# A graph-convolution kernel on one core: a 23rd tile slot, one buffer of x instead of two, and the kept tiles stated per column band

## What is computed

```python
A = adj + eye(8192)
deg = sum(A, axis=1)
d = rsqrt(deg)
h = (A * d[:, None] * d[None, :]) @ x
out = layernorm(x + elu(h @ w))
```

## Time and profile before

| | |
|---|---|
| median of three runs | 1066.4 us |
| the profiled execution's own time | 1068.32 us |
| its span on the core | 1066.5 us |
| TensorE (PE) busy | 926.0 us, 87% |
| VectorE (DVE) busy | 765.1 us, 72% |
| ScalarE (ACT) busy | 711.9 us, 67% |
| read from HBM | 364.2 MB, 345 GB/s over the span |
| loads of adj | 338, of 1 MB each, all by SyncE's queue (SP) |
| loads of x into the scaling buffer | 21 |

### The profile page before, as it was taken

How to read it: one execution, slowest core, us unless ns; L and a number is a source line. 1 busy time by engine, 2 the same in 40 slices (tenths; PEclk the granted TensorE clock), 3 DMA queues, 4 the chain that set the end, 5 groups by cost and what they waited for, 6 DMA issues and landing times.

```text
span 1066.5 us, 35050 instructions
## 1 busy us (share of the span) xinstructions
PE 926.0 (87%) x15744; PEld 846.4 (79%) x15744; DVE 765.1 (72%) x633; ACT 711.9 (67%) x1693; POOL 196.2 (18%) x268
## 2 busy tenths in 40 slices
PE   0089399499597998998989899999999999999995
PEld 0086189399596997798889888979989999999994
DVE  0587587566766767787777677989998785866933
ACT  6898898888988889898988979850226828100201
POOL 0210120300402103041230444474001100000000
PEclk9999799699898999999899999999999999999998
DMA  9999999999999999999999999979997998999930
GB/s 378 397 387 412 395 397 403 394 398 401 397 397 400 393 377 400 379 395 389 389 391 374 394 394 345 337 257 372 302 301 268 287 304 278 291 328 311 357 111 21
DMA packets 170903, 370.66 MB, mean 348 GB/s; under 512 B 6272, under 2 KB 33536, under 8 KB 161536
## 3 DMA queue, kind: packets, MB, share of 16 engines
q1 hardware_dynamic: 153856, 360.01, 91.7%
q10 hardware_dynamic: 16896, 8.39, 2.7%
HBM read 364.18 MB, written 4.19 MB: 345 GB/s over the span
## 4 chain that ended last, share of the span: by engine, by line
PE 45%; issue 40%; DMA 6%; POOL 5%; ACT 2%; DVE 1%; SPq 1%; POOLq 0%; DVEq 0%; ACTq 0%
PE p_set L883 44%; DMA space<-in_adj 6%; POOL space L769 3%; ACT space L786 1%; PE p_set L861 1%; DMA xn<-in_x 1%; POOL xn L762 1%; POOL rstd L776 1%; POOL space L750 0%; SPq L731 0%; POOL d L756 0%; DVE space L914 0%; ACT space L794 0%; DVE hT L925 0%; ACT L786 0%
## 5 line engine op out<-in xcount | busy, mean ns | idle before, releaser
L883 PE MATMUL p_set<-space 32*128 32x256 f32 (+2 forms) x15616 | 909.6, 391 | 127.3 <-ACT space L794 61.0
L883 PEld LDWEIGHTS p_set<-space 32*128 32x128 f32 x15616 | 831.0, 188 | 201.6 <-issue 144.9
L901 DVE STREAM_TRANSPOSE space<-space 128x2048 f32<-128x2048 f32 x256 | 582.2, 2296 | 119.4 <-ACT space L786 75.1
L786 ACT ACTIVATE space<-space 128x512 f32<-128x512 f32 (+2 forms) x744 | 578.7, 779 | 82.8 <-DMA space<-in_adj 78.8
L925 DVE TENSOR_TENSOR hT<-p_set,hT 128x1024 f32<-128x1024 f32 (+1 forms) x108 | 104.2, 986 | 136.0 <-PE p_set L883 135.9
L809 ACT ACTIVATE space<-space 128x512 f32<-128x512 f32 x16 | 10.1, 629 | 199.9 <-DVE space L936 199.8
L786 ACT ACTIVATION_READ_ACCUMULATOR space<-space 128x1 f32 x744 | 138.9, 187 | 0.0
L769 POOL COPY space<-xn 32x512 f32<-32x512 f32 x192 | 120.5, 628 | 11.9
L756 POOL TENSOR_TENSOR d<-deg,half 128x4 f32<-128x4 f32 x16 | 16.3, 1018 | 542.6 <-DVE deg L907 542.6
L794 ACT ACTIVATE space<-xn 32x512 f32<-32x512 f32 x112 | 70.3, 627 | 43.9 <-POOL xn L762 35.3
L776 POOL TENSOR_TENSOR rstd<-var_eps,half 128x4 f32<-128x4 f32 x16 | 16.5, 1031 | 279.8 <-DVE var_eps L970 279.7
(11 more groups left out here) (16 smaller groups left out, 29.8 us busy)
## 6 DMA issues: line engine op xcount, KB each, us to landing
space<-in_adj SPq DMA_DIRECT2D x338, 1024.0 KB, 13.0
xn<-in_x SPq DMA_DIRECT2D x21, 256.0 KB, 12.7
space<-in_x ACTq DMA_DIRECT2D x16, 256.0 KB, 5.8
out_rows<-space ACTq DMA_DIRECT2D x16, 256.0 KB, 7.3
w_sb<-in_w SPq DMA_DIRECT2D x1, 64.0 KB, 1.8
```

The lines of the kernel that those rows point to most:

```text
L786: ins = nc.scalar.activation(view[:, g], view[:, g], ACT.Copy, accum_out=to[:, g:g + 1])
L883: ins = nc.tensor.matmul(to, xs_chunk(h, j)[quadrant(q)], moving, start=first and s == b == 0, stop=last and s == b == 3)
L901: nc.vector.transpose(slots[slot], slots[slot]).then_inc(tile_turned, 1)
```

## The change

The planner's constants and two places of the program change:

- SLOTS 22 to 23, and XN 2 to 1: one more slot of 8 KB per partition, one buffer of x (2 KB per partition) less.
- The kept tiles are stated per column band, always the ones nearest the diagonal. It adds tiles (6,2), (6,3) and (8,5): 57 kept instead of 54, so 79 tiles are loaded again instead of 82.
- WIDTHS (2,) to (4, 2): a group of four kept tiles side by side, loaded in four pieces of 128 rows x 2048 columns, where five slots are free and four of them adjacent.
- STAY 11 to 10 (band 10 keeps its home; homes are loaded 20 times, not 21), FEED 12 to 14, FLIGHT 5 to 4, and the costs that the planner counts with.
- w is loaded over the identity matrix, before the ninth "again" tile, when all 16 diagonals are done (`sp.wait_ge(diagonal_added, BANDS)`), no longer first of all; TensorE waits for it before the first product with w.

```diff
-SLOTS = 22
+SLOTS = 23
-KEEP = (12, 10, 8)
+KEPT = (1, 2, 3, 4, 5, 6, 5, 4, 4, 4, 5, 4, 1, 2, 3, 4)
-STAY = 11
-WIDTHS = (2,)
-XN = 2
+STAY = 10
+WIDTHS = (4, 2)
+XN = 1
-FEED = 12
-FLIGHT = 5
+FEED = 14
+W_AFTER = 8
+FLIGHT = 4
...
 def kept_units():
+    return {(t, u) for t in range(BANDS) for u in range(t + 1 - KEPT[t], t + 1)}
...
-    FAR, NEAR, XLOAD, LAND = 2.5, 2.68, 0.9, 2.0
+    FAR, MID, NEAR, XLOAD, LAND = 2.57, 2.65, 2.73, 1.0, 2.0
...
-            offer("pool", 3, "scale", home_of[t], 1.35)
+            offer("pool", 3, "scale", home_of[t], 1.15)
...
-                offer(e, 0 if some is FIRST_COPIES else 4, "copies", (arg, i), {"dve": 0.43, "act": 0.64, "pool": 0.8}[e] * len(pairs))
+                offer(e, 0 if some is FIRST_COPIES else 4, "copies", (arg, i), {"dve": 0.65, "act": 0.64, "pool": 0.72}[e] * len(pairs))
...
-                    kind, long = "part", took(len(parts[arg][2]))
+                    kind, long = "part", took(len(parts[arg][2])) + (1.75 if now - until["pe"] > 2.5 else 0.0)
...
-        w_sb = sb("w_sb", [F, F])
+        w_sb = ident
...
-            sp.dma_start(w_sb[:, :], w).then_inc(w_loaded, 16)
+            agains = [arg for what, arg in order["sp"] if what == "load" and loads[arg][:2] == ("tile", "again")]
             for what, arg in order["sp"]:
+                if what == "load" and arg == agains[W_AFTER]:
+                    sp.wait_ge(diagonal_added, BANDS)
+                    sp.dma_start(w_sb[:, :], w).then_inc(w_loaded, 16)
...
                 elif kind == "copies":
                     h, some = arg
                     pool.wait_ge(x_scaled, scale_nth[h])
+                    diagonals_before = sum(k == "diagonal" for k, _ in order["pool"][:order["pool"].index((kind, arg))])
+                    if diagonals_before:
+                        pool.wait_ge(diagonal_added, diagonals_before)
...
-            pe.wait_ge(w_loaded, 16)
             for kind, arg in order["pe"]:
                 if kind == "out":
+                    if not arg:
+                        pe.wait_ge(w_loaded, 16)
```

More of the change, by code:

```diff
@@ L261, in issue @@
             wide = load[5] * (BAND if load[0] == "near" else 1) if load[0] != "tile" else BAND
-            dma = max(dma, now + 1.0) + (FAR if wide == 2048 else NEAR - 0.1 if wide >= 1024 else NEAR)
+            dma = max(dma, now + 1.0) + (FAR if wide == 2048 else MID if wide >= 1024 else NEAR)
             events.append((dma + LAND, k, "landed", k))
@@ L321, in finished @@
             known.add(arg)
-            offer("pool", 0, "scale", home_of[arg], 1.35)
+            offer("pool", 0, "scale", home_of[arg], 1.15)
             if arg in held_diagonals:
```

## The result

The changed kernel takes 1060.79 us (median of seven runs, 1058.63 to 1063.25) against 1066.40 us: ratio 0.996, interval 0.9947 to 0.9972. It is faster by 4.3 us by the ratio and by 5.6 us by the medians, where 11.9 were forecast. The profiled execution took 1063.25 us, the slowest of the seven, with a span of 1061.5.

The account below looks back on a forecast made before the run. Loads were taken to bound the kernel until 596 us, TensorE afterwards. 1068.3 - 10.4 (kept tiles) - 1.5 (wide pieces) = 1056.4 us for the profiled execution, 1.9 us over the median, so 1054.5 us was forecast, range 1042 to 1071.

Parts of the forecast that it names:

- The reading of the bound: Whole kernel: loads set the pace until 596 us, then TensorE alone; its work left at the last wait sets the end.
- the walked start of band 9: TensorE, band 9: starts at 596.6 us, without a wait and without the slow clock.
- the walk: TensorE's timeline, bands 6 to 9, with three more kept tiles: followed band by band, 10.4 us saved.
- The buffer of x: Loads of x, end of pass one: at most 25 us late, hidden by TensorE's backlog, cost 0.
- the 10.4 counted for them: Bands 6 and 8: three more kept tiles, multiplied before band 9, save 10.4 us.
- First product with w after 749: nothing.: Pass two: w's later load, behind an "again" load issued at about 734.5 us, costs nothing.
- the loads unmoved: Before band 8: d at 549.32 us and home 8 not ready before 555.29, loads taken as unmoved.
- Cost **0: Slots while strips 2 to 7 pass: one slot less shortens the load queue from five to four, cost 0.
- the wait that was forecast before band 8: TensorE before band 8: wait grows from 2.76 to 4.2 us and the slow clock stays, 3.1 us.
- The wide pieces: Near loads before band 9: up to 32 wide pieces, 0.09 us each, at most 2.9 us; 1.5 us taken.
- I take 0, between +5 and the gain of the first rival: Load order: FEED, FLIGHT, STAY and the planner's costs only reorder loads; effect taken as 0.
- the first rival: Waits after band 4: all five go with their slow clock, 24.2 us gained, 1042 us; chance 0.13.

Follow-up runs that it names:

- w_front: The changed kernel with w in a place of its own, loaded first of all, queue orders unchanged: 1057.67 us, ratio 0.9914 to the kernel before.
- before_x1: The kernel before with one buffer of x in the program alone, order still planned for two: 1084.14 us, ratio 1.0159.
- w_front_kept54: w_front with the 54 kept tiles of the kernel before, order planned anew: 1067.55 us, ratio 1.0039 to the kernel before.
- narrow_held: w_front with each group of four wide pieces loaded as four single tiles, same order and slots: 1060.82 us, ratio 0.9963 to the kernel before.
- w_later: The changed kernel with W_AFTER 12 instead of 8, so w goes out four loads later: 1073.62 us, ratio 1.0063 to the kernel before.

## Why the prediction was wrong

**What held.** The reading of the bound: what TensorE has left at its last wait sets the end. At 596.85 us, 0.3 after the walked start of band 9, TensorE had done what the walk gave it and 32 matmuls (1.7 us) more, and w_front, the change without its late w, measured 0.9914, 9.2 us (7.7 to 10.6) of the 11.9. The buffer of x is hidden at the end of pass one (TensorE full from 596.85 to 740.4 us, and before_x1's first window). Taking the tiles away (w_front_kept54) costs 13 us by the ratios and 8.7 by the spans, on either side of the 10.4 counted for them, with waits before bands 7 and 9 where the walk had them, though in another plan.

**The step that failed** is the one on w: "First product with w after 749: nothing." Two things were wrong in it. It compared 749 with 734.5, the time at which w would be *issued*, and left out the landing, although 14.1 us of it stood two paragraphs above. And it took the first product's time from the kernel before, although the change itself makes that product earlier. Issue at 734.5 and a landing some 9 to 14 us later, against a product due near 740, would have given the wait. It is 3.97 us and 2.97 more at the slow clock, 6.9 in the profile, 4.9 by the ratios of the changed kernel and w_front.

**Where the walk came out right for another reason.** Bands 5 and 6 began at 405.64 and 463.23, 2.5 us late each, against "the loads unmoved". d of row bands 5 and 6 came 2.8 and 3.3 us later, at 401.94 and 457.67. The loads of that stretch waited more for TensorE's slots: between 343 and 460 us SyncE waits 32.4 us for its matmuls in the kernel before (first line) and 85.4 in the changed one; in w_front_kept54, with 54 tiles, it is 36.5. The wait before band 5 grew from 2.96 to 4.63 us, and from 403 to 460 us the DMA engines moved 369 GB/s instead of 391. So the "Cost **0**" of the slots was wrong by some 3 us at band 6. By d of band 9, at 591.62 in w_front and 586.39 in w_front_kept54, the three tiles hold the loads up by some 5 us, if the new plan isn't at fault.

```profile
SPq L731 <- PE p_set L883: 32.4, 10, 7.5
```

```profile
SPq L725 <- PE p_set L881: 85.4, 15, 9.4
```

The cost went into the wait that was forecast before band 8 (4.2 us and 3.1 of slow clock), which turned out at 0.42, 0.65 and 0.67 us with the clock at full speed. Band 7 ended 2.4 us later than walked, and home 8 could be used 1.4 us earlier: d of band 8 came at 549.38 against 549.32, as forecast, but VectorE made its copies (line 912, before 914) without an addition to hT ahead of them.

```profile
553.74 1.41 DVE L914 COPY space<-xn 32x512 f32<-32x512 f32 x2
```

```profile
551.55 2.22 DVE L912 COPY space<-xn 32x512 f32<-32x512 f32 x2
```

That the walk still met the measured time at band 9 is luck in part: the 2.4 us of late start fell into a wait that was expected anyway, and the 3.1 us of slow clock behind it didn't come.

**Sizes.** The lone parts, which odd numbers of kept tiles bring, were not counted: five at 0.23, 1.2 us. The wide pieces were put at 1.5, of up to 32 pieces (strip 6, with five near tiles, was left out of the count); twelve came about. narrow_held has 2 us for these twelve against single tiles, but d of bands 1 to 4 in the changed kernel stand at 127.97, 203.39, 272.78 and 339.43 against 129.10, 202.70, 273.54 and 339.18 before, so nothing was left of it by band 4; that the slots took it is likely and not shown. The Trainium skill's rule weighed in the prediction (DMA: Bandwidth & Descriptors, Specifications: line rate from 512 B on) does not describe this: 404 and 390 GB/s for 8 KB and 2 KB rows in one place of one queue.

**The reordering.** "I take 0, between +5 and the gain of the first rival" fits this plan, though no run measures the order alone, and is far too narrow as a bound for plans near it: 3% for FEED and FLIGHT, 5.5% for three tiles with a slot less.

## What to carry to other kernels

When a load is moved from the front of a queue to the middle, date its *landing*, behind what is queued ahead of it, against its first use in the *changed* kernel; a small late constant belongs on a queue of its own. When one resource is traded for another (a slot for a buffer), test the order together with it: each half alone, in a plan of its own, was worthless or harmful here. And where a hand-made plan sets the order, undo one part with the order held, or the experiment measures the new plan.

## What the runs showed of the chip

64 KB took 13.7 us (11.7 in w_later) from issue to landing on SyncE's queue behind loads of 1 MB, and 5.8 us on ScalarE's at the same time of the kernel. After a wait of 3.97 us for w TensorE's granted clock stood at 0.50 (1.2 GHz; the first eight matmuls in 2.08 us instead of 1.16), and so it did after one of 13.23 us; but the part behind the long wait lost less (7.95 us) than the one behind the short wait (9.24). In these two executions the loss did not grow with the wait: about four us after TensorE went on the clock was still at 0.50 behind the short wait, and back at 1.00 behind the long one.

```profile
748.00:750.00 2.00, 2.00 (x25) 1.63 (x24) 2.00 (x1) 0.47 (x1) 0.00 (x0) 0.50 1.05 387
```

```profile
758.00:760.00 2.00, 2.00 (x44) 1.82 (x40) 2.00 (x2) 0.30 (x1) 0.00 (x0) 1.00 0.00 0
```
